# Four layers over eight images: from image by image to stage by stage, attention as one stream of 96 heads

## What is computed

```
x = x + L0(gn(x))   # A: attention, 12 heads of 16, rope on q and k, biases
x = x + L1(gn(x))   # B: convolution, selective scan in 4 directions, gate
x = x + L2(gn(x))   # C: attention, 12 heads, relative position bias in h and w, biases
x = x + L3(gn(x))   # D: attention in a 7x7 neighbourhood, 12 heads
```

## Time and profile before

| | |
|---|---|
| median of 3 runs | 9161.37 us (9146.53 to 9166.74) |
| profiled execution, its own time | 9161.64 us |
| its span | 9159.8 us, 102914 instructions |
| PE busy | 7055.3 us, 77% |
| PE weight loads busy | 2817.0 us, 31% |
| DVE busy | 5434.8 us, 59% |
| ACT busy | 3152.0 us, 34% |
| POOL busy | 1101.3 us, 12% |
| mean granted clock of PE | 0.861 of full |
| DMA | 298.58 MB, mean 33 GB/s |

### The profile page before, as it was taken

The page is one execution under the profiler, slowest core; times in us unless marked ns, Lnnn a source line. Parts: engine busy times, 40 slices in busy tenths (PEclk is TensorE's granted clock), DMA queues, the critical chain, the costliest instruction groups (busy, mean ns, idle before and its releaser), DMA issues.

```text
span 9159.8 us, 102914 instructions
## 1 busy us (share of the span) xinstructions
PE 7055.3 (77%) x32648; PEld 2817.0 (31%) x32648; DVE 5434.8 (59%) x5732; ACT 3152.0 (34%) x3418; POOL 1101.3 (12%) x412
## 2 busy tenths in 40 slices
PE   6779777797777977779777797767977779776797
PEld 2233322333223332233322333223332233322333
DVE  6675466654666546675376653766537665376653
ACT  3424334243342433324333243332433324333242
POOL 0230002300023000230002300022000220003200
PEclk9889888898888988889888898888988879888798
DMA  2001110011100111001110011100111001110011
GB/s 64 8 26 36 44 47 7 26 35 44 47 7 27 35 46 47 6 28 34 47 46 5 28 34 48 45 5 28 34 48 45 5 28 34 50 43 5 28 34 51
DMA packets 158947, 298.58 MB, mean 33 GB/s; under 512 B 48974, under 2 KB 56390, under 8 KB 158378
## 3 DMA queue, kind: packets, MB, share of 16 engines
q1 hardware_dynamic: 158378, 291.44, 10.6%
HBM read 185.75 MB, written 83.50 MB: 29 GB/s over the span
## 4 chain that ended last, share of the span: by engine, by line
PE 50%; DVE 19%; issue 9%; DMA 7%; ACT 6%; SPq 4%; DVEq 4%; POOL 1%; ACTq 0%; POOLq 0%
PE px L607 9%; PE ring L557 7%; PE ring L584 6%; PE ring L560 4%; DVE hs L1265 4%; ACT pt L677 3%; DMA ks<-k_split 3%; PE ring L586 3%; PE ring L1010 3%; PE px L1025 3%; DVE rq L748 2%; PE ring L985 2%; PE ring L536 2%; PE ring L476 2%; DVE hs L1254 2%
## 5 line engine op out<-in xcount | busy, mean ns | idle before, releaser
L763 DVE TENSOR_REDUCE mx<-ring 128x1 f32<-128x1024 f32 (+1 forms) x1920 | 2177.4, 1141 | 1536.9 <-PE ring L560 873.4
L677 ACT ACTIVATE pt<-ring 128x1024 f32<-128x1024 f32 (+1 forms) x1920 | 1857.4, 980 | 2591.0 <-PE ring L586 1146.7
L557 PE MATMUL ring<-kb,qb 96*128 96x512 bf16 x3072 | 1137.6, 414 | 285.5 <-DVE rq L748 172.7
L607 PE MATMUL px<-pt,vo 128*32 128x512 f32 (+3 forms) x8064 | 1192.6, 581 | 71.4 <-ACT pt L677 71.3
L1310 POOL TENSOR_TENSOR hc<-hs,crep 128x1024 f32<-128x1024 f32 x384 | 1044.6, 2720 | 1525.3 <-DVE hs L1265 1480.8
L584 PE MATMUL ring<-qb,kb 99*128 99x512 bf16 x3072 | 1077.8, 394 | 44.4 <-DVE nb L783 42.0
L1265 DVE TENSOR_TENSOR_SCAN hs<-ring,hs 128x1024 f32<-128x1024 f32 x384 | 874.5, 2277 | 1.5 <-ACT ring L1158 1.5
L1010 PE MATMUL ring<-duh,spread 96*128 96x512 f32 x1536 | 632.1, 523 | 289.9 <-DVE hs L1254 164.1
L560 PE MATMUL ring<-hot,rq 128*128 128x512 f32 x1536 | 844.3, 612 | 0.0
L831 POOL TENSOR_TENSOR ocm<-ocm,rb 96x1024 f32<-96x1024 f32 x24 | 56.5, 2354 | 6509.2 <-DMA rb<-reciprocals 6509.2
L586 PE MATMUL ring<-rq,hot 128*128 128x512 f32 x1536 | 821.1, 597 | 0.0
(11 more groups left out here) (153 smaller groups left out, 6519.3 us busy)
## 6 DMA issues: line engine op xcount, KB each, us to landing
qs<-q_split SPq DMA_DIRECT2D x192, 128.0 KB
q_parts<-part SPq DMA_DIRECT2D x96, 192.0 KB, 3.5
k_parts<-part SPq DMA_DIRECT2D x96, 192.0 KB, 2.7
qb<-q_parts SPq DMA_DIRECT2D x192, 96.0 KB
kb<-k_parts SPq DMA_DIRECT2D x192, 96.0 KB
ocm<-os SPq DMA_DIRECT2D x576, 32.0 KB
rb<-reciprocals SPq DMA_DIRECT2D x288, 64.0 KB, 2.2
qb<-q_parts SPq DMA_DIRECT2D x192, 64.0 KB
```

Source lines behind the costliest of these rows:

```text
L557: last = nc.tensor.matmul(out[:, half], m.qb[u][0:BR, q], m.kb[u][0:BR, half], start=True, stop=L == "A")
L607: last = nc.tensor.matmul(m.px[32 * g:32 * g + 32, h % 2, lo - f * HF:hi - f * HF], m.vo[:, t, h, :], pt[:, lo - q0:hi - q0], start=t == t ...
L677: nc.scalar.activation(pt, ps, ACT.Exp, scale=1.0 if L == "C" else HD ** -0.5).then_inc(s.pt, 1)
L763: nc.vector.tensor_reduce(out, ps, AX.X, ALU.max).then_inc(s.mx_used, 1)
```

## The change

The loop over images is gone. The program is written out stage by stage: A for all eight images, then B, C, D; between stages x stands in DRAM (`m.xd`), and two buffers `m.x` take images in turn. At the start of a stage every engine waits until the last x of the stage before is stored (`begin`).

Attention is one stream of 96 heads per layer. A table (`agenda`) says at which turn n of the stream the steps of image i + 1's prologue and of image i - 1's tail are done; `AHEAD` counts turns back from the image's first unit, `JOB_LAGS` are the turns between the steps of a job, `BEHIND` counts turns after the last. Jobs, rotations, V products (4 tiles of tokens a unit), statistics' sums and projections are units of the same ring of three slots.

The steps are divided anew: ACT makes the upper parts (`top`, `mid`) and copies V out; POOL multiplies with the cosine and scales both halves of the output; DVE keeps turn, sum, rest and low. The V bias is folded into the projection bias at the start. V stands in rows of 17 columns per head in place of 32 (32 columns are still loaded as weights). The relative products of C take the three bf16 parts (`qb`, 96 rows) in place of two f32r parts (48 rows), so C no longer writes and reads these; its k is scaled by scaled weights. The rows of D's mask are loaded once. Heads' loads have one semaphore per buffer. At the start, the relative tables are split into three bf16 parts.

```diff
-    m.vo = sb(ctx, "vo", [P, NT, NH, VC])
...
+        m.vo = [sb(attn, f"vo{i}", [P, NT, NH * VW + VC - VW]) for i in range(2)]
...
+    m.qkd = nc.dram_tensor("qk_split", (2, 2, 2, C, N), F32, kind="Internal").ap()
+    m.qkp = nc.dram_tensor("qk_parts", (2, 2, 3, C, N), BF16, kind="Internal").ap()
+    m.xd = {L: nc.dram_tensor(f"x_{L}", (B, NC, CP, N), F32, kind="Internal").ap() for L in LAYERS[:-1]}
...
+def begin(eng, m, L):
+
+    if L != LAYERS[0]:
+        eng.wait_ge(m.i.x_out, 16 * turns(L, 0))
+
...
+def load_image(sp, m, L, img, src):
+
+    if img >= 1:
+        sp.wait_ge(m.i.x_in, 16 * turns(L, img))
+    if img >= 2:
+        sp.wait_ge(m.i.x_out, 16 * (turns(L, img) - 1))
+    sp.dma_start(m.x[img % 2][:], src[img:img + 1].rearrange("a c p n -> p (a c) n")).then_inc(m.i.x_in, 16)
+
...
+         "D": dict(norm=27, jobs=(32, 35, 38, 41), tokens=(34, 37))}
...
+            "D": dict(job=0, top=0, low=0, part=1)}
...
+          "D": dict(reciprocal=13, back=13, spread=13, normal=13, proj=20)}
...
+        for i, n in enumerate(ahead["jobs"]):
+            for kind, lag in JOB_LAGS[L].items():
+                put(start + n + lag, kind, img, i)
+        for i, n in enumerate(ahead["tokens"]):
+            put(start + n, "tokens", img, i)
+        for c, end in ((0, size * img + lead + 7 * STEPS[L] - behind["reciprocal"]), (1, size * (img + 1))):
+            for kind in ("reciprocal", "back", "spread", "normal"):
+                put(end + behind[kind], kind, img, c)
+        for c in range(NC):
+            put(size * (img + 1) + behind["proj"] + c, "proj", img, c)
+        put(size * (img + 1) + behind["proj"] + 2, "leave", img)
+    return plan
...
-    units = []
-    for n in range(UNITS[L] + LEAD[L]):
+    units, plan = [], agenda(L)
+    total, lead = per_image(L) * B, LEAD[L]
+    for n in turns_of(L, plan):
+        for unit in plan.get(n, []):
+            if unit[0] in ("sums", "job", "rot", "tokens", "proj"):
+                units.append(unit)
...
+            elif old[0] == "rot":
+                pe.wait_ge(s.turned, 4 * old[1] + old[2] + 1)
+            elif old[0] == "proj":
+                pe.wait_ge(m.i.x_done, NC * turns(L, old[1]) + old[2] + 1)
...
-        qs = m.qs[h % NBUF]
+        qb = m.qb[h % NBUF]
         for r in range(H):
-            q = qs[0:QR, r:N:W] if axis else qs[0:QR, r * W:(r + 1) * W]
+            q = qb[0:BR, r:N:W] if axis else qb[0:BR, r * W:(r + 1) * W]
...
+    def top(img, i):
+
+        used = 2 * img + i // 2
+        if used:
+            act.wait_ge(s.stored[i % 2], JOB_OUT[L] * used)
+        if L == "A":
+            act.wait_ge(s.rotated, 4 * img + i + 1)
+            nc.scalar.activation(m.part[i % 2][:, 0, :], m.raw[i % 2][:], ACT.Copy).then_inc(a.top, 1)
...
+    def cosine(img, i):
+
+        raw = m.raw[i % 2][:]
+        pool.wait_ge(s.rot_ps, 4 * img + i + 1)
+        nc.gpsimd.tensor_tensor(raw, raw, m.cos[:], ALU.mult).then_inc(s.cosine, 1)
...
-    for h in range(NH):
-        if h + 1 < NH:
-            maxima(h + 1)
-        if h >= 1:
...
-        if h + NBUF < NH:
-            sp.wait_ge(s.st_ps, total * b + steps * (h + 1))
-            load(h + NBUF)
...
+    jobs = 0
+    for n in turns_of(L, plan):
+        for kind, img, i in plan.get(n, []):
+            if kind == "part":
+                part(img, i)
+                jobs += 1
+                if img == 0 and i == 1:
+                    for h in range(NBUF):
+                        load(h, jobs)
+            if kind == "back":
+                back(img, i)
+            if kind == "spread":
+                spread(img, i)
+            if kind == "leave":
+                store_image(sp, m, L, img, x_to)
+                if img + 2 < B:
+                    load_image(sp, m, L, img + 2, x_from)
+        if maxima_ready(L, n):
+            maxima(n // steps - 1)
+        h, left = divmod(n - lead, steps)
+        if left == 0 and 1 <= h and h - 1 + NBUF < NH * B:
+            sp.wait_ge(s.st_ps, steps * h)
+            load(h - 1 + NBUF, jobs)
+        if left == 2 and 1 <= h <= NH * B:
```

992 lines of the change are left out of this document (558 added, 434 removed).

## The result

The changed kernel takes **8866.71 us** (median of 4 runs, 8860.77 to 8883.91), the kernel before 9153.95 us beside it (4 runs, 9140.33 to 9166.74): ratio **0.969**, 95% interval 0.9668 to 0.9711. It is faster by 287 us, where 783 were forecast; the time lies outside the range of 8060 to 8670. The profiled execution took 8870.59 us, its span is 8868.8.

The account below looks back on a forecast made before the run. PE and the three-slot ring were taken to pace A and C, with borders where PE mostly waits. A -343, C -355, D -133, B 0, stage borders +40 and start +8 sum to -783 from 9161.6: 8379 us, range 8060 to 8670.

Parts of the forecast that it names:

- Start, +8: Program start: six more constants to load and a three-way split of the tables cost about 8 us more.
- A, 45 us an image in the stream: A's borders: 33.4 us of inserted PE work plus 11.6 for DVE passes (bounds 0 and 27) per image.
- the same work in the same order ... 0: Scan B: unchanged at 320.4 us an image, so no gain or loss.
- C, head 24.21 less 27 us in all: C's heads: 24.21 us each as before, with bf16 relative products saving 27 us over the stage, a quarter of 104.
- bounds 0 to 17, taken 6, since DVE idles 43%: C's borders: DVE passes moved into the stream add 6 us an image to 26.5 of PE work, making 32.5.
- the loop of 12.3: D's heads: scores, maxima transfers, then the next head's load close a loop of 12.3 us a head, above PE's 6.44.
- Bounds 0 and about 30; I take 15: D's borders: crowded jobs, V products and SP's extra transfers stretch the loop by 15 us an image.
- (1): D: the loop does not close because loads arrive sooner; total 8101, or 7931 at PE's pace; chance 0.15.
- (2): D: waits send PE to its low clock, so inserted work takes 53 us an image; +276, total 8655; chance 0.11.
- (3): A and C: DVE's passes are all on the path and bf16 products gain nothing; +212, total 8591; chance 0.10.
- (4): A and C: waits inside a job's chain stop the stream as long as the old borders; +668, total 9047; chance 0.02.
- (5): C's dense PE stream: the unrolled program starves PE of instructions; at 2 us a packet +1138, total 9517; chance 0.02.

Follow-up runs that it names:

- b_pool_late: The changed kernel with a one-column GpSimd memset ahead of GpSimd's product at nine tiles of each image in B: 8748.7 us.
- short_passes: The changed kernel with DVE's turn, sum, rest and low passes in A and C cut to 128 of 1024 columns: 8746.7 us.
- d_load_first: The changed kernel with each head's load in D issued on SyncE ahead of the maxima, not behind them: 8731.5 us.
- d_half_work: The changed kernel with D's jobs and V products multiplying only the first 96 of 192 channels: 8816.8 us.
- c_pool_turns: The changed kernel with GpSimd copying each head's q by image columns in C, so the second relative product reads neighbouring columns: 8723.8 us.

## Why the prediction was wrong in size

- **Direction and mechanism** were right: the borders of A and C lie within the stream, their prologues vanish but for the first, and so do the transfers between layers but for three.
- **What failed** is the size of four terms: B taken as unchanged (107 us short), the heads of C taken as cheaper (160 of C's 228), and the borders of C and of D taken at 32.5 and 15 us. Their causes follow.
- **Start, +8:** measured +14.7. The passes came as forecast: SyncE issues the first x at 43.21 us in place of 36.93. The rest was left out of the sum: the second x and both rope tables are now issued ahead of the first statistics, which wait 5.67 us for the sine table, the last of them, where before they waited 5.79 for x alone.
- **A, 45 us an image in the stream:** measured 222.0 - 12 x 13.86 = 55.7 between later images (227 - 166 = 61 in the first two). By the windows of a plain head and of a period:

```profile
531.57:545.43 13.86, 12.41 (x65) 3.11 (x66) 11.27 (x14) 8.57 (x10) 0.00 (x0) 1.00 0.12 35
...
854.12:1076.11 221.99, 191.50 (x880) 54.92 (x879) 161.71 (x191) 117.68 (x126) 14.09 (x6) 0.95 0.16 48
```

PE is busy 191.5 in the period against 12 x 12.41 in plain heads, so 42.6 us of PE where "33.4 us that stay on PE's path" stood, and 13 us of idling where 11.6 stood. The passes were sized about rightly; PE's records were priced at full clock, and the period has 0.95. The border's 10.7 us too little are 75 us over seven images; the head's 14.20, which came out at 13.86, gave 33 back, and that A missed by 46 only is luck.
- **B, "the same work in the same order ... 0":** the step that failed by its principle. Order on each engine was the same, order *between* two engines was decided by 0.1 us and turned round. +107 us; b_pool_late gives 116 back. By its own sign "B at 320 us an image" this part was wrong.
- **C, head 24.21 less 27 us in all:** measured 25.6. "I take a quarter" had the right sign for neighbouring columns and the wrong one for the strided group. No row showed a bf16 product over strided columns, and I had bounded the price by 0 from below where a loss should have been allowed. The clock nearly doubled it (1.0 us a head by itself, 1.9 more in every second). 96 x 1.7 = 160 of the 228 us.
- **C, "bounds 0 to 17, taken 6, since DVE idles 43%":** 352.5 - 12 x 25.6 = 45 us an image where 32.5 stood. That is near 26.5 + 17, but by luck. The window of a period:

```profile
5432.96:5784.51 351.55, 320.65 (x2016) 140.29 (x2014) 183.72 (x206) 138.76 (x146) 4.73 (x2) 0.91 0.11 30
```

PE is busy 320.65 us against 12 x 23.79 in plain heads, so 35 us where 26.5 stood, and it idles 30.9 against 12 x 1.83, so 9 us where 6 stood. The larger part of the miss is again PE's work at a lower clock (0.91), and short_passes shows the two tied: 7.8 us of passes taken off gave 3.2 us of idling and 3.9 of busy time. A share of idle time says little about what a pass costs.
- **D, the loop of 12.3:** right to a tenth, and d_load_first confirms its parts. **"Bounds 0 and about 30; I take 15":** 28. The upper end was nearer, in part for the reason that I named (crowding) and then discounted: d_half_work gives 6.5 us of it back, the rest stays open. D's 1451 us lie just outside the 1250 to 1450 that I had set as a condition.
- **Handovers, 13.3 each:** the vector engine waits 9.9, 0 and 1.6 us at them; with the drains they are hard to separate, and small.
- **Rivals.** (1) fell: D's loop closes (and the 9.4 us a head that it took from the rows are 9.5: 19.03 / 2). (2) is right about the clock of D (0.80; the border head at 0.62 lies near the lower level); its price of 276 us is more than the whole miss of D, 98, and what part of these is the clock no run shows. (3) had the passes' price nearly right for C, half for A, though partly by the clock. (4) and (5) fell with the total. The Trainium skill's floor for small matmuls (TensorE: Matmul & The Clock Gate, "Wait — 56ns, not 53.3ns?"), about 25 ns, was not reached: c_pool_turns shows 32 in 0.97 us, 30 ns each, and a gain of 0.43 us a head, 41 us, under the 55 that it allowed.
- The range held cases that each moved one term. Here all moved the same way: B and C's heads beyond bounds that held no loss, the borders of A, C and D toward the upper ends of bounds of which I had taken the middle or less, with no price for the clock of the inserted work.
